# Eight row scatters behind the second routing half, and the v projection of the next chunk moved up behind q

## The chip, the cores and the metric

The program runs on one core of a Trainium2 chip. Its five instruction queues are TensorE (PE in the profile, PEld for its weight loads), VectorE (DVE), ScalarE (ACT), GpSimd (POOL) and SyncE (SP); they meet only at semaphores. The time is the device time of one execution in microseconds (us).

## The reference

The inputs are 8 sequences of 512 tokens with 256 features (4096 tokens). Each token is layer-normalised to `xn`. From it come two branches:

```
q, v   = xn @ Wq, xn @ Wv
state  = lam * state_before + v          # along the 512 tokens, lam = sigmoid(beta) per head
y      = layernorm(q * state) * ln_g + ln_b
s      = (y * silu(xn @ Wg)) @ Wo

logits = xn @ router.T                   # 8 experts, the best 2 of a token, softmax of the two
moe    = sum over the 2 experts e of gate_e * (silu(a) * b) @ w_out[e].T,  a, b = halves of xn @ w_in[e].T
out    = x + s * silu(moe + bias)
```

## The kernel before, in words

The work has three stages, each with its own instruction order per engine, written out by hand.

**Stage 1, normalise and route (0 to about 45 us).** The 8 sequences ("chunks") are normalised, transposed and projected on the 8 experts. The choice of two experts is made in two halves of 16 token tiles each: `choose(0)` on VectorE after chunks 0 to 3, `choose(1)` after chunks 4 to 7. Behind each choice, TensorE counts ranks (`count_ranks`), and VectorE turns them into a row number for every (token, expert) pair (`count`, `place`). `place(g)` signals `routed`; `choose(g)` signals `chosen_ready`.

**Stage 2, the recurrence (about 45 to 173 us).** It goes chunk by chunk, c = 0 to 7. VectorE runs the scan of v along the tokens (L910, signals `states_ready`), splits pieces of the expert weights (L919), multiplies by q (L923, signals `prod_ready`), multiplies by the gate (L954, L960), and takes the statistics of q * state (L936, L943, signals `y_var`). GpSimd makes the reciprocal standard deviation from them (`rstd`, L414 to L417, signals `y_rstd`). ScalarE normalises with it (L646, signals `z_ready`). TensorE transposes the result (`transpose_z`, L1134), ScalarE applies ln_g and ln_b (L605), and one chunk later the gate and the output projection follow (`project_out`). TensorE's accumulators are fixed: bank A holds v, bank B holds q, bank C the gate and the output projection by turns, bank D the transposes. So v of chunk c + 1 may be written only when the scan of chunk c has read bank A.

Beside this, GpSimd copies all token rows to their places in a list sorted by expert in DRAM: 64 scatters (L452), each of 128 rows, one for a token tile and one of its two experts. They are issued from GpSimd's own queue in batches between the calls of `rstd`: `SCATTERS_FIRST` of them ahead of chunk 0, then `SCATTERS_EACH` = 8 behind the `rstd` of each chunk, until 64 are out:

```
            done = SCATTERS_FIRST
            scatter(0, done)
            for c in range(CH):
                if c >= 1:
                    pool.wait_ge(z_ready, c)
                rstd(0, y_var, c + 1, y_rstd)
                end = min(done + SCATTERS_EACH, N_SCATTERS)
                scatter(done, end)
                done = end
```

With 14 first, chunks 0 to 5 carry 8 each, chunk 6 carries the last 2, and chunk 7 none. `scatter` waits for `routed` of the half that its rows belong to.

**Stage 3, the experts (from about 173 us).** SyncE waits until all 64 scatters have landed (`rows_scattered`) and loads the sorted rows block by block (L347). TensorE transposes a block (L1192), and runs the two layers of its expert as products of fp16 pieces (L1068, the helper `three`, which also makes all projections of stage 2). The results are scattered back with an add (L525), and after the last block the chunks are finished and stored.

Of the kernel before, what the change touches and what calls it, by code (L numbers as in the profile page):

```python
# [62 lines left out]
GROUPS = 2  # L63
# [4 lines left out]
MASKED = -3.0e38  # L68
ROWS_OUT = T + P
N_SCATTERS = TOPK * NT  # L70
SCATTERS_FIRST = 14
SCATTERS_EACH = 8


# [27 lines left out]
def build(nc, x, wq, wv, wg, wo, beta, ln_g, ln_b, router, w_exp, bias, out):  # L102
    ctx = ExitStack()
    with ctx:
# [84 lines left out]
        def routing(shape, dims, dt=F32, words=None):  # L189
# [46 lines left out]
        bankA, bankB, bankC, bankD = [  # L236
            ctx.enter_context(nc.psum_tensor(f"bank{n}", [P, 2, 512], F32)) for n in "ABCD"]
# [14 lines left out]
        def slots_ps_of(b, i):  # L252
# [13 lines left out]
        logits_done, route_step, chosen_ready, ranks_done = map(  # L266
            sem, ("logits_done", "route_step", "chosen_ready", "ranks_done"))
# [3 lines left out]
        v_ps, q_ps, g_ps, yt_ps, zt_ps, o_ps = map(  # L271
            sem, ("v_ps", "q_ps", "g_ps", "yt_ps", "zt_ps", "o_ps"))
        states_ready, prod_ready, ybn_done, y_var, y_rstd, z_ready = map(
            sem, ("states_ready", "prod_ready", "ybn_done", "y_var", "y_rstd", "z_ready"))
# [112 lines left out]
        def _(pool):  # L387
# [59 lines left out]
            def scatter(first, end):  # L447
                for a in range(first, end):
                    slot, row = scatters[a]
                    if a % (TOPK * GT) == 0:  # L450
                        pool.wait_ge(routed, a // (TOPK * GT) + 1)
                    pool.indirect_dma_start(  # L452
                        out=slots_dram, out_offset=bass.IndirectOffsetOnAxis(slot, 0),
                        in_=row, in_offset=None,
                        bounds_check=SLOTS - 1, oob_is_err=False).then_inc(rows_scattered, 16)


            done = SCATTERS_FIRST
            scatter(0, done)
            for c in range(CH):  # L460
# [87 lines left out]
        def _(act):  # L548
# [50 lines left out]
            def affine(c, buffers=early_buffers):  # L599
                _, w, _, _ = buffers  # L600
                act.wait_ge(zt_ps, c)
                if not isinstance(c, int) or c >= 2:
                    act.wait_ge(p_lo_ready, KD * (c - 1))
                for m in range(KD):
                    act.activation(w[:, m, :], bankD[:, m, :], ACT.Identity, bias=cols[:, 2, m:m + 1],  # L605
                                   scale=cols[:, 1, m:m + 1]).then_inc(w_ready, 1)

            def split_p(c, buffers=early_buffers):
                _, w, p_hi, _ = buffers
                if not isinstance(c, int) or c >= 2:  # L610
                    act.wait_ge(o_ps, c - 1)
                for m in range(KD):
                    act.wait_ge(p_ready, KD * (c - 1) + m + 1)
                    act.activation(p_hi[:, m, :], w[:, m, :], ACT.Copy).then_inc(p_hi_ready, 1)
# [105 lines left out]
        def _(dve):  # L720
# [181 lines left out]

            def recur(c, convert=True):
                states, _, _, _ = early_buffers
                later = not isinstance(c, int) or c >= 1
                dve.wait_ge(v_ps, c + 1)
# [156 lines left out]
        def _(pe):  # L1063
# [38 lines left out]
            def project_half(bank, a, c, m):  # L1102
                return three(bank[:, m, :], range(KD),
                             lambda k: wat_hi[:, a, k, m * P:m * P + P],
                             lambda k: wat_lo[:, a, k, m * P:m * P + P],
                             lambda k: xnT[:, bass.ds(c, 1), k, :].rearrange("p a n -> p (a n)"),
                             lambda k: xnT[:, bass.ds(c, 1), KD + k, :].rearrange("p a n -> p (a n)"))

            def project(bank, a, c):
                project_half(bank, a, c, 0)  # L1110
                return project_half(bank, a, c, 1)
# [18 lines left out]
            def transpose_z(c):  # L1130
                pe.wait_ge(z_ready, c)
                for j in range(TPC):
                    for m in range(KD):
                        last = pe.transpose(bankD[:, m, j * P:j * P + P], z[:, j, m * P:m * P + P],  # L1134
                                            ident32[:, :])
                last.then_inc(zt_ps, 1)

            def project_out(c):
                _, _, p_hi, p_lo = early_buffers
                pe.wait_ge(p_lo_ready, KD * c)  # L1140
                for j in range(TPC):
                    last = three(bankC[:, j // 2, j % 2 * D:j % 2 * D + D], range(KD),
                                 lambda k: p_hi[:, k, j * P:j * P + P],
                                 lambda k: p_lo[:, k, j * P:j * P + P],
                                 lambda k: wat_hi[:, 3, k, :],
                                 lambda k: wat_lo[:, 3, k, :])
                last.then_inc(o_ps, 1)

            def recur(c, last=False):

                states, _, _, _ = early_buffers
                later = not isinstance(c, int) or c >= 1
                if later:
                    pe.wait_ge(prod_ready, c)
                project(bankB, 0, c).then_inc(q_ps, 1)
                if later:
                    transpose_z(c)
                if not isinstance(c, int) or c >= 2:
                    pe.wait_ge(s_ready, c - 1)
                if later:  # L1160
                    project(bankC, 2, c).then_inc(g_ps, 1)
                pe.wait_ge(prod_ready, c + 1)
                if later:
                    pe.wait_ge(w_ready, KD * c)
                for j in range(TPC):
                    for m in range(KD):
                        y_t = pe.transpose(bankD[:, j // 2, j % 2 * D + m * P:j % 2 * D + m * P + P],  # L1167
                                            states[:, m, j * P:j * P + P], ident32[:, :])
                y_t.then_inc(yt_ps, 1)
                if not last:  # L1170
                    pe.wait_ge(states_ready, c + 1)
                    project(bankA, 1, c + 1).then_inc(v_ps, 1)
                if later:
                    pe.wait_ge(gate_ready, c + 1)
                    project_out(c)

            project(bankA, 1, 0).then_inc(v_ps, 1)
            count_ranks(1)
            repeat(pe, 1, CH - 1, 1, recur)
            recur(CH - 1, last=True)  # L1180


# [148 lines left out]
```

## Time and profile before

| what | us |
|---|---|
| median of 3 runs (lowest, highest) | 524.18 (521.8, 524.3) |
| the profiled execution, its own time | 526.04 |
| its span in the trace | 524.3 |
| TensorE busy in the span | 431.1 (82%) |
| VectorE busy | 305.7 (58%) |
| GpSimd busy | 273.8 (52%) |
| ScalarE busy | 214.8 (41%) |

All times of rows count from the start of the span. A row of the timeline gives the start, the busy time, the engine, the source line, the operation, what it writes and reads, and in brackets how long the engine sat idle ahead of it and what released it. "issue" means that nothing in the profile released it, "remote" that a semaphore rose with no instruction's end beside it. Line numbers are those of the kernel before; in the changed kernel the lines behind L457 stand one to four lines lower.

### The profile page before, as it was taken

To read this page: it belongs to the slowest core of one execution; us is meant where nothing else is said; L and a number is where in the kernel's file an instruction comes from. 1 tells how busy PE (TensorE), PEld (TensorE's weight loads), DVE (VectorE), ACT (ScalarE), POOL (GpSimd) and SP (SyncE) were. 2 spreads that over 40 slices of the span, in tenths; PEclk is the share of its full clock that TensorE was granted. 3 is DMA by queue.
4 is the path that set the end of the run, shared out by engine and by line. 5 is a ranking of instruction groups with operands and counts; after the bars stand their busy time and mean duration, and the time that the engine had idled before them with its cause. 6 is when DMAs were issued, how large, how long until landed. Compare 5 with 4: busy or idle time off the path is not lost.

```text
span 524.3 us, 12044 instructions
## 1 busy us (share of the span) xinstructions
PE 431.1 (82%) x3446; PEld 339.5 (65%) x3447; DVE 305.7 (58%) x589; ACT 214.8 (41%) x340; POOL 273.8 (52%) x524
## 2 busy tenths in 40 slices
PE   1766389699699989999899998999999999998000
PEld 1643245465355878888798887888888888765000
DVE  4897489889687445454445453545545454444067
ACT  4872136558565534243323333333434243232050
POOL 4716377477885206555555655564646556543300
PEclk9999689799899999999999999999999999999755
DMA  7802143996892224565434333434334343442398
GB/s 252 301 12 83 61 163 139 316 290 231 280 325 96 66 81 62 141 140 106 61 57 63 68 50 62 70 59 71 52 69 60 61 60 57 68 64 30 71 334 306
DMA packets 52692, 64.70 MB, mean 123 GB/s; under 512 B 5552, under 2 KB 47536, under 8 KB 52656
## 3 DMA queue, kind: packets, MB, share of 16 engines
q1 hardware_dynamic: 37712, 45.55, 28.1%
q0 software_dynamic: 13296, 17.83, 20.3%
q10 hardware_dynamic: 1664, 1.06, 0.7%
q8 instruction: 10, 0.16, 0.1%
q14 instruction: 10, 0.08, 0.0%
HBM read 40.02 MB, written 28.74 MB: 131 GB/s over the span
## 4 chain that ended last, share of the span: by engine, by line
PE 48%; DMA 13%; DVE 11%; issue 11%; POOL 8%; ACT 3%; another core or an unknown queue 2%; SPq 2%; DVEq 0%; POOLq 0%; ACTq 0%
PE bankC L1068 16%; PE bankB L1068 14%; PE bankA L1068 14%; DMA y_dram<-rows_raw 8%; POOL slots_dram L452 4%; PE bankD L1192 3%; DMA w_raw<-x_in 2%; DMA rows_raw<-slots_dram 2%; DMA w_raw<-y_dram 1%; DVE w_raw L919 1%; POOL stat L416 1%; DVE work L910 1%; DVE w_raw L1046 1%; DVE bn L735 1%
## 5 line engine op out<-in xcount | busy, mean ns | idle before, releaser
L525 POOL DMA_INDIRECT y_dram<-rows_raw x71 | 113.3, 1596 | 31.3 <-issue 31.3
L1068 PE MATMUL bankC<-w_raw,rows_raw 128*128 x852 | 99.6, 273 | 2.2 <-DVE rows_raw L1038 2.2
L1068 PEld LDWEIGHTS bankC<-w_raw,rows_raw 128*128 128x128 f16 x852 | 82.0, 98 | 14.0 <-issue 3.3
L1068 PE MATMUL bankA<-rows_raw,w_raw 128*128 128x256 f16 x768 | 89.1, 273 | 1.2 <-DVE rows_raw L975 1.2
L1068 PE MATMUL bankB<-rows_raw,w_raw 128*128 128x256 f16 x768 | 89.1, 273 | 0.0
L452 POOL DMA_INDIRECT slots_dram<-rows_raw,pos_i x64 | 72.1, 1127 | 31.2 <-issue 20.7
L1068 PEld LDWEIGHTS bankA<-rows_raw,w_raw 128*128 x768 | 75.0, 98 | 10.1 <-issue 1.4
L1068 PEld LDWEIGHTS bankB<-rows_raw,w_raw 128*128 x768 | 75.2, 98 | 8.3
L985 DVE TENSOR_TENSOR rows_raw<-rows_raw 128x512 f16<-128x512 f32 x64 | 44.3, 692 | 45.6 <-ACT rows_raw L673 45.6
L981 DVE SCALAR_TENSOR_TENSOR rows_raw<-rows_raw,bankA 128x512 f32<-128x512 f32 x32 | 22.0, 688 | 73.6 <-ACT rows_raw L668 73.6
L673 ACT ACTIVATE rows_raw<-rows_raw 128x512 f16<-128x512 f32 x64 | 40.3, 630 | 49.7 <-DVE rows_raw L981 49.7
L668 ACT ACTIVATE rows_raw<-bankA 128x512 f32<-128x512 f32 x32 | 19.1, 597 | 101.0 <-PE bankA L1068 67.6
L519 POOL TENSOR_TENSOR spare<-spare 128x1 f32<-128x1 f32 x32 | 6.2, 194 | 94.0 <-DVE rows_raw L1000 93.0
L1000 DVE TENSOR_SCALAR rows_raw<-bankC,rows_raw 128x256 f32<-128x256 f32 x71 | 31.4, 479 | 11.3 <-DMA y_dram<-rows_raw 9.3
L981 DVE SCALAR_TENSOR_TENSOR rows_raw<-rows_raw,bankB 128x512 f32<-128x512 f32 x32 | 22.0, 688 | 15.0 <-ACT rows_raw L668 15.0
L668 ACT ACTIVATE rows_raw<-bankB 128x512 f32<-128x512 f32 x32 | 19.1, 597 | 21.3 <-PE bankB L1068 21.3
L919 DVE SCALAR_TENSOR_TENSOR w_raw<-work,w_raw 128x1024 f32 (+1 forms) x24 | 27.7, 1216 | 0.0
L646 ACT ACTIVATE work<-bankD,stat 128x256 f32<-128x256 f32 x32 | 15.4, 565 | 23.7 <-POOL stat L417 23.6
L975 DVE TENSOR_TENSOR rows_raw<-bankD,rows_raw 128x512 f16<-128x512 f32 (+1 forms) x37 | 23.4, 633 | 2.5 <-ACT rows_raw L660 2.4
L618 ACT ACTIVATE w_raw<-work 128x1024 f32 (+1 forms) x24 | 23.5, 1046 | 1.9 <-DMA work<-w_exp_in 1.9
L1167 PE MATMUL bankD<-ident,work 128*128 128x128 f32 x64 | 10.5, 317 | 16.5 <-DVE work L923 16.5
L1192 PE MATMUL bankD<-ident,rows_raw 128*128 128x128 f32 x134 | 21.5, 278 | 3.1 <-DMA rows_raw<-slots_dram 3.0
(180 smaller groups left out, 664.5 us busy)
## 6 DMA issues: line engine op xcount, KB each, us to landing
work<-w_exp_in SPq DMA_DIRECT2D x24, 512.0 KB
rows_raw<-slots_dram SPq DMA_DIRECT2D x32, 260.0 KB
w_raw<-x_in SPq DMA_DIRECT2D x9, 512.0 KB, 4.2
y_dram<-bias_in SPq DMA_DIRECT2D x4, 1024.0 KB
w_raw<-y_dram SPq DMA_DIRECT2D x8, 512.0 KB, 7.3
out<-w_raw SPq DMA_DIRECT2D x8, 512.0 KB, 3.7
work<-x_in SPq DMA_DIRECT2D x7, 512.0 KB
slots_dram<-fill SPq DMA_DIRECT2D x9, 260.0 KB
```

Of the source, the lines that this page charges most:

```text
L452: pool.indirect_dma_start(out=slots_dram, out_offset=bass.IndirectOffsetOnAxis(slot, 0), in_=row, in_offset=None, bounds_check=SLOTS - 1, ...
L525: pool.indirect_dma_start(out=y_dram, out_offset=bass.IndirectOffsetOnAxis(to, 0), in_=ys[i][:, s, :], in_offset=None, bounds_check=ROWS_O ...
L618: act.activation(w_hi[:, bass.ds((c * PIECES + i) * PIECE, PIECE)], wst[:, i % STAGES, :], ACT.Copy, scale=WSCALE).then_inc(w_hi_ready, 1)
L668: act.activation(sil[j][:, :, 0:n], AB[j][:, :, 0:n], ACT.Silu, scale=1.0 / WSCALE).then_inc(sil_ready, 1)
L673: act.activation(g_hi[i][:, 2 * j:2 * j + 2, 0:n], g32[j][:, :, 0:n], ACT.Copy)\
L919: dve.scalar_tensor_tensor(w_lo[:, piece], wst[:, i % STAGES, :], WSCALE, w_hi[:, piece], ALU.mult, ALU.subtract).then_inc(w_lo_ready, 1)
L975: dve.tensor_tensor(xT[i][:, KD:2 * KD, 0:n], slots_ps_of(b, i)[:, :, 0:n], xT[i][:, 0:KD, 0:n], ALU.subtract).then_inc(slot_lo_ready, 1)
L981: dve.scalar_tensor_tensor(g32[j][:, :, 0:n], sil[j][:, :, 0:n], 1.0 / WSCALE, AB[j][:, :, BLOCK:BLOCK + n], ALU.mult, ALU.mult).then_inc( ...
L985: dve.tensor_tensor(g_lo[i][:, 2 * j:2 * j + 2, 0:n], g32[j][:, :, 0:n], g_hi[i][:, 2 * j:2 * j + 2, 0:n], ALU.subtract).then_inc(g_split, 1)
L1000: last = dve.tensor_scalar(ys[i][:, s, :], bankC[:, i, s * D:s * D + D], gates[:, s:s + 1], None, ALU.mult)
L1068: last = pe.matmul(out_ap, lhsT, rhs, start=(n == 0), stop=(n == len(todo) - 1))
L1192: last = pe.transpose(slots_ps_of(b, i)[:, k, s * P:s * P + P], slot_in[i][:, s, k * P:k * P + P], ident32[:, :])
```

## The change

Two places are edited. GpSimd waits for `chosen_ready` of both halves before its first scatter, and issues 8 instead of 14 there. On TensorE, the v projection of chunk c + 1 stands directly behind the q projection of chunk c, ahead of the transposes of z, the gate's projection and the transposes of q * state; before it stood behind all three.

```diff
-SCATTERS_FIRST = 14
+SCATTERS_FIRST = 8
 SCATTERS_EACH = 8
...
+            pool.wait_ge(chosen_ready, GROUPS)
             done = SCATTERS_FIRST
             scatter(0, done)
...
                 project(bankB, 0, c).then_inc(q_ps, 1)
+                if not last:
+                    pe.wait_ge(states_ready, c + 1)
+                    project(bankA, 1, c + 1).then_inc(v_ps, 1)
                 if later:
                     transpose_z(c)
...
                 y_t.then_inc(yt_ps, 1)
-                if not last:
-                    pe.wait_ge(states_ready, c + 1)
-                    project(bankA, 1, c + 1).then_inc(v_ps, 1)
                 if later:
                     pe.wait_ge(gate_ready, c + 1)
                     project_out(c)
```

GpSimd's queue around the first scatters and the first two chunks, before (`slots_dram` is the sorted list, `mv` and `stat` the statistics of a chunk, `x13` a run of like instructions):

```order
L452 DMA slots_dram<-rows_raw,pos_i 35072x260 [waits routed]
L452 DMA slots_dram<-rows_raw,pos_i 35072x260 x13
L414 TENSOR_SCALAR stat<-mv 128x4 [waits y_var]
L415 TENSOR_SCALAR stat<-mv 128x4
L416 TENSOR_TENSOR stat<-stat,neg_half 128x4 [waits pool_step]
L417 TENSOR_TENSOR stat<-stat 128x4 [waits pool_step]
L452 DMA slots_dram<-rows_raw,pos_i 35072x260 x8
L414 TENSOR_SCALAR stat<-mv 128x4 [waits y_var,z_ready]
```

And in the changed kernel:

```order
L452 DMA slots_dram<-rows_raw,pos_i 35072x260 [waits routed,chosen_ready]
L452 DMA slots_dram<-rows_raw,pos_i 35072x260 x7
L414 TENSOR_SCALAR stat<-mv 128x4 [waits y_var]
L415 TENSOR_SCALAR stat<-mv 128x4
L416 TENSOR_TENSOR stat<-stat,neg_half 128x4 [waits pool_step]
L417 TENSOR_TENSOR stat<-stat 128x4 [waits pool_step]
L452 DMA slots_dram<-rows_raw,pos_i 35072x260 x8
L414 TENSOR_SCALAR stat<-mv 128x4 [waits y_var,z_ready]
```

The first batch has one more wait and six scatters fewer; every later scatter moves back by six places, and the batch behind the `rstd` of chunk 6 grows from 2 to 8.

TensorE's queue in chunk 0, from the last q product on, before (bank B is q, bank A is v, bank D takes the transposes, `xs_raw` is the transposed input, `work` holds q * state):

```order
L1068 MATMUL bankB<-xs_raw,wat_hi 128x512 x2
L1068 MATMUL bankB<-xs_raw,wat_lo 128x512
L1167 MATMUL bankD<-ident,work 128x128 [waits prod_ready]
L1167 MATMUL bankD<-ident,work 128x128 x7
L1068 MATMUL bankA<-xs_raw,wat_hi 128x512 [waits states_ready]
L1068 MATMUL bankA<-xs_raw,wat_hi 128x512
L1068 MATMUL bankA<-xs_raw,wat_lo 128x512
```

And in the changed kernel, where the source lines have shifted:

```order
L1069 MATMUL bankB<-xs_raw,wat_hi 128x512 x2
L1069 MATMUL bankB<-xs_raw,wat_lo 128x512
L1069 MATMUL bankA<-xs_raw,wat_hi 128x512 [waits states_ready]
L1069 MATMUL bankA<-xs_raw,wat_hi 128x512
L1069 MATMUL bankA<-xs_raw,wat_lo 128x512
```

The 12 products of v(1) now follow those of q(0) and wait only for the scan; the 8 transposes, which wait for `prod_ready`, come behind them. In the loop over chunks 1 to 6 the same move is made past the transposes of z, the 12 products of the gate and the transposes of q * state.

## Rows read from the trace of the kernel before

**Rows 1.** Engine busy times by stretch: from:to, length, busy (instructions), PEclk, DMA, GB/s.

```profile
190.00:206.00 16.00, 16.00 (x147) 14.26 (x146) 7.34 (x13) 4.76 (x8) 6.83 (x15) 1.00 0.37 92
```

**Rows 2.** GpSimd's timeline: the scatters and the first rstd instruction of chunks.

```profile
40.86 1.26 POOL L452 DMA_INDIRECT slots_dram<-rows_raw,pos_i  x1 [10.55 <-DVE rows_raw L812]
...
57.80 0.98 POOL L452 DMA_INDIRECT slots_dram<-rows_raw,pos_i  x1 [0.30 <-issue]
66.50 0.24 POOL L414 TENSOR_SCALAR stat<-mv 128x4 f32<-128x4 f32 x1 [7.72 <-DVE mv L943]
...
80.89 0.24 POOL L414 TENSOR_SCALAR stat<-mv 128x4 f32<-128x4 f32 x1 [0.39 <-issue]
...
100.52 0.24 POOL L414 TENSOR_SCALAR stat<-mv 128x4 f32<-128x4 f32 x1 [5.92 <-DVE mv L943]
...
116.35 0.24 POOL L414 TENSOR_SCALAR stat<-mv 128x4 f32<-128x4 f32 x1 [1.89 <-DVE mv L943]
...
152.39 1.97 POOL L452 DMA_INDIRECT slots_dram<-rows_raw,pos_i  x1 [0.30 <-issue]
...
161.30 0.24 POOL L414 TENSOR_SCALAR stat<-mv 128x4 f32<-128x4 f32 x1
...
163.79 1.10 POOL L452 DMA_INDIRECT slots_dram<-rows_raw,pos_i  x1 [0.54 <-issue]
165.19 0.97 POOL L452 DMA_INDIRECT slots_dram<-rows_raw,pos_i  x1 [0.30 <-issue]
```

**Rows 3.** VectorE's timeline, stages 1 and 2.

```profile
39.70 0.17 DVE L812 TENSOR_SCALAR rows_raw<-w_raw 128x16 f32<-128x16 f32 x1
...
45.27 0.42 DVE L770 TENSOR_REDUCE w_raw<-bankD 128x128 f32<-128x256 f32 x1 [2.77 <-remote]
...
54.51 0.17 DVE L844 TENSOR_TENSOR_SCAN w_raw<-w_raw 128x8 f32<-128x8 f32 x1
61.19 1.22 DVE L923 SCALAR_TENSOR_TENSOR work<-bankB,work 128x1024 f32<-128x1024 f32 x1 [6.51 <-remote]
...
66.13 0.28 DVE L943 BATCH_NORM_AGGREGATE mv<-bn 128x2 f32<-128x6 f32 x3
68.40 2.33 DVE L910 TENSOR_TENSOR_SCAN work<-cols,bankA 128x512 f32<-128x512 f32 x2 [1.99 <-PE bankA L1068]
...
102.30 2.33 DVE L910 TENSOR_TENSOR_SCAN work<-cols,bankA 128x512 f32<-128x512 f32 x2 [1.95 <-PE bankA L1068]
...
150.04 4.61 DVE L919 SCALAR_TENSOR_TENSOR w_raw<-work,w_raw 128x1024 f32 x4
...
164.84 1.22 DVE L923 SCALAR_TENSOR_TENSOR work<-bankB,work 128x1024 f32<-128x1024 f32 x1 [2.44 <-PE bankB L1068]
```

**Rows 4.** TensorE's timeline, the products whose ends others wait for.

```profile
42.55 0.56 PE L1087 MATMUL bankD<-rt,xs_raw 128*128 128x16 f16 x16 [0.29 <-DVE xs_raw L746]
...
54.15 0.38 PE L1068 MATMUL bankB<-xs_raw,wat_lo 128*128 128x512 f16 x1
...
104.61 0.27 PE L1068 MATMUL bankC<-wat_hi,work 128*128 128x256 f16 x1
```

**Rows 5.** ScalarE's timeline, the copy of the output projection of chunk 2.

```profile
107.46 1.02 ACT L623 ACTIVATE xs_raw<-bankC 128x1024 f32 x1 [3.03 <-remote]
```

**Rows 6.** SyncE's timeline: issue of the first two block loads.

```profile
168.46 1.55 SPq L347 DMA_DIRECT2D rows_raw<-slots_dram  x2
```

**Rows 7.** The chain of waits: 12 projection products, one block load (start, us, what).

```profile
104.89 2.59 PE bankB L1068 x12
...
313.98 2.72 DMA rows_raw<-slots_dram
```

**Rows 8.** TensorE's timeline: the first block's transposes and its first expert product.

```profile
172.83 1.04 PE L1192 MATMUL bankB<-ident,rows_raw 128*128 128x128 f32 x8
175.06 0.61 PE L1068 MATMUL bankA<-rows_raw,w_raw 128*128 128x256 f16 x4 [1.19 <-DVE rows_raw L975]
```

**Rows 9.** Engine busy times by stretch, behind TensorE's wait for q * state.

```profile
61.20:66.00 4.80, 3.53 (x13) 2.37 (x14) 4.62 (x16) 0.00 (x0) 0.00 (x0) 0.50 0.00 0
```

## The prediction

> **What bounds the kernel now.** I read the busy times by stretch first, then the timelines of GpSimd, VectorE and TensorE for stages 1 and 2. In stage 3 TensorE is busy without a gap, 16.00 of 16.00 us [rows 1], and neither edit touches it. So the question is only when stage 3 starts: its first expert product is at 175.06 [rows 8].
>
> In stage 2, GpSimd is the engine to follow. Call R(c) the start of the `rstd` of chunk c. R(0) to R(3) are 66.50, 80.89, 100.52 and 116.35, and R(6) is 161.30 [rows 2]. In front of R(2) and R(3) GpSimd stood idle for 5.92 and 1.89 us, released by VectorE's statistics. In front of R(1) the idle time is 0.39 us, and R(6) shows none: there the eight scatters of the chunk before set the pace. From R(3) to R(6), 44.95 us, I take it that scatters set it.
>
> The start is set by something else. The statistics of chunk 0 end at T0 = 66.13 + 0.28 = 66.41 [rows 3], and two waits ahead of them are marked "remote". Routing L770 starts at 45.27 although its last product ended at 42.55 + 0.56 = 43.11 [rows 3, 4]: 2.2 us late. The product L923 starts at 61.19, although VectorE was free at 54.68 and the last q product ended at 54.53 [rows 3, 4]: 6.7 us after it. By the code L923 waits for nothing but q and the scan, so TensorE's signal itself arrived late. The only other work that runs through both waits is the 14 scatters, 40.86 to 58.78 [rows 2], and L923 starts 2.4 us after the last one was issued. A third case is ScalarE's copy at 107.46, 2.6 us behind a product that ended at 104.88 [rows 4, 5], also among scatters. But L923 of chunk 7 starts 0.0 us after the q product that released it, with a scatter running at 163.79 [rows 2, 3]. So scatters go with late signals, but not always. In the two shorter cases TensorE had more work queued behind the signal; in the 6.7 us case its next instruction waited for VectorE.
>
> **The change, part by part.**
>
> *No scatters during the second choice.* L770 can start at about 43.2, 2.1 us earlier, and everything behind it on VectorE moves along: the choice, which ended at about 50.0, ends at 47.9, and VectorE is free for L923 at 54.68 - 2.1 = 52.6 instead of 61.19. GpSimd's first scatter began 0.99 us after its release (39.70 + 0.17 to 40.86 [rows 2, 3]), so the new first one begins at 48.9. The pace is (57.80 - 40.86) / 13 = 1.30 us; eight take 7 x 1.30 + 0.98 = 10.1, with 0.3 for the longer first, to 59.3.
>
> *T0.* With no late signal, L923 moves from 61.19 to 52.65, and T0 from 66.41 to 57.9. But q of chunk 0 now ends inside the scatters again. The lower bound of the lateness is 0 (chunk 7), the upper one is "2.4 us after the last scatter", L923 at 61.7. I take one delay of 2.4 us, the mean of 2.2 and 2.6, because v(1) now stands behind q(0) on TensorE, as other work did in the two shorter cases. T0 = 60.3. GpSimd is then free at 59.3, so it does not bind.
>
> *v moved up.* VectorE's scan waited 1.99 us at 68.40 and 1.95 at 102.30 for v [rows 3], because v stood behind the transposes. Now v is ready when VectorE gets there, and both waits go. What is late next? R(1) follows from the scatters, R(0) + 14.4. R(2) follows from VectorE: before 100.52 = T0 + 34.1, now T0 + 32.1; scatters would allow T0 + 28.2 (94.60 - 66.41). R(3) was T0 + 49.9, now less both waits, T0 + 46.0; scatters give T0 + 32.1 + 13.9 = T0 + 46.0, the same. From there the scatters set the pace, and a further wait removed is worth nothing: R(6) = T0 + 46.0 + 44.95 = T0 + 91.0, against T0 + 94.9 before.
>
> What stands behind the moved v on TensorE is the transposes of z. If v waits for the scan, they wait too: 2.6 us for v [rows 7], 1.04 for the transposes [rows 8], 0.8 on ScalarE, 4.4 in all behind the scan. VectorE needs the result only after L919 and L923, 4.61 + 1.2 = 5.8 us behind the same scan [rows 3]. The cover is 1.4 us, so I price the move at zero; a TensorE at half clock would use the cover up and cost about 2 us in that chunk, which GpSimd's pace mostly hides from chunk 3 on.
>
> *Six scatters moved back.* Before, chunk 6 carried two, and the last was issued by S = 165.19 + 0.97 = 166.16. Now it carries eight: 2.49 us of `rstd` (161.30 to 163.79) and 10.1 of scatters, so S = R(6) + 12.6 = T0 + 103.6, against T0 + 99.75. The block loads wait for it: SyncE issued the first 2.30 us after S [rows 6], and a load takes 2.7 us [rows 7], so TensorE transposes block 0 from S + 5.0, and the first expert product follows as before 2.1 us behind the end of waiting: S + 7.1 = T0 + 110.7. Before it was T0 + 108.65, and the loads were then hidden by the recurrence. So at an unchanged T0 this part costs 2.0 us: 3.9 from v gained, 5.9 lost to the scatters.
>
> A rule bears on the moved scatters. The scatter at 152.39 took 1.97 us instead of 0.98, beside L919 on VectorE from 150.04 for 4.61 us [rows 2, 3]. The Trainium skill (SBUF — State Buffer, section "SBUF: two separate sides") says that GpSimd and a VectorE instruction with two SBUF inputs lock each other out of a shared port pair for a whole instruction. By it, the six scatters leave a stretch where VectorE has little of that kind and enter chunk 7, where L954 and L960 are such instructions. The sum would be some 1 us worse if one scatter there doubles; chunk 7 has no L919, and I leave it out.
>
> *Clock.* TensorE now runs out of work at R(6) + 11.5 (172.83 - 161.30), T0 + 102.5, and gets block 0 at T0 + 108.6, an idle stretch of 6.1 us that was not there. After the idle stretch behind q(0) it was granted 0.50 of its clock, the 1.2 GHz level [rows 9]. Bounds: 0, or the transposes and the first 24 products (1.04 + 24 x 0.11 = 3.6, by four of them in 0.61 us, the last taking 0.27 [rows 8]) at double time, 3.6 us. I take 1.5, nearer the lower end, since these products also wait for copies on ScalarE and VectorE.
>
> **Sum.** T0 60.3 - 66.4 = -6.1; scatters against v +2.0; clock +1.5. Total -2.6 us. The profiled execution's own time is 526.04, 1.9 above the median of 524.18: I expect 523.4 for an execution like it, and 524.18 - 2.6 = 521.6 for the median.
>
> **Rivals.**
> - *No signal is late any more* (scatters in a row of eight leave TensorE's signals alone, as in chunk 7). T0 = 57.9, so -8.5 + 3.5 = -5.0: 519.2. Against it: two of three late signals came with fewer than eight scatters out.
> - *The signal waits for the end of the scatters.* L923 at 61.7, 0.5 later than before, T0 66.9, so +0.5 + 3.5 = +4.0: 528.2. For it: the 6.7 us case ended only once the scatters were out. This path is slower from T0 = 62.9 on, that is, when the signals cost over 5.0 us.
> - *The late signals have nothing to do with scatters.* Then L770 and L923 stay where they are and only the 3.5 us of the other parts remain: 527.7.
> - *The last batch hides after all* (clock at no cost, loads faster): -2.6 - 2.0: 519.6.
>
> **How the numbers follow.** Chances: forecast 0.42, no lateness 0.20, end of the scatters 0.23, no link 0.08, hidden batch 0.07. The forecast's own range is 519.5 to 524, by its clock bounds and a delay of 0 to 4 us. About 0.5% (2.6 us) is what a measurement of this kernel can tell from no change, and the forecast lies on that edge: half of it counts as faster. Faster 0.21 + 0.20 + 0.06 = 0.47; slower: most of the two cases above 527, 0.24; the same 0.29. The range is 518.0 to 528.3, which leaves out little more than the tails of the rivals.
>
> **What would show it.** Right: L770 within 0.2 us of its last product; L923 between 52.6 and 56; no wait of L910 for bank A; R(3) to R(6) still about 45 us; eight scatters behind R(6); a new TensorE idle stretch of some 6 us ahead of the first block's transposes, with SyncE's loads directly behind the last scatter. Wrong: L923 still near 61 us, or the block loads issued before TensorE ends the recurrence, which would mean that GpSimd does not set the end of stage 2.

## The result, and the profile after

Over 20 executions of each kernel the median went from 524.07 to 525.34 us; the ratio is 1.0055, 95% interval 1.0029 to 1.008. The two medians alone give 1.0024 and the two means 1.0044, so the size of the loss is known only roughly; its interval leaves out 1. Ratios leave out executions of a slower state, the medians given here keep them. The forecast was 521.6: the change is slower, not faster. The profiled execution of the changed kernel took 524.37 us (span 522.6), against 526.04 and 524.3 for the one that the prediction was worked out from. That pair says -1.7 where the medians say +1.3, so one pair of profiles does not settle it. The times of before lie in two groups (518.8 to 520.5 and, mostly, 523 to 526.5), those of the changed kernel between 522 and 527.7.

GpSimd's timeline in the changed kernel: first and last scatter of the first batch, R(0), R(2), R(3), R(6), last scatter of all.

```profile
48.77 1.26 POOL L452 DMA_INDIRECT slots_dram<-rows_raw,pos_i  x1 [18.39 <-DVE w_raw L782]
...
58.14 0.97 POOL L452 DMA_INDIRECT slots_dram<-rows_raw,pos_i  x1 [0.30 <-issue]
59.18 0.24 POOL L414 TENSOR_SCALAR stat<-mv 128x4 f32<-128x4 f32 x1
...
92.17 0.24 POOL L414 TENSOR_SCALAR stat<-mv 128x4 f32<-128x4 f32 x1 [3.91 <-DVE mv L944]
...
106.50 0.24 POOL L414 TENSOR_SCALAR stat<-mv 128x4 f32<-128x4 f32 x1
...
150.55 0.24 POOL L414 TENSOR_SCALAR stat<-mv 128x4 f32<-128x4 f32 x1
...
162.49 0.97 POOL L452 DMA_INDIRECT slots_dram<-rows_raw,pos_i  x1 [0.30 <-issue]
```

VectorE's timeline there: first routing step of the second half, product of chunk 0, end of its statistics, and the gate product of chunk 2.

```profile
43.06 0.42 DVE L771 TENSOR_REDUCE w_raw<-bankD 128x128 f32<-128x256 f32 x1 [0.65 <-PE bankD L1088]
...
52.59 1.22 DVE L924 SCALAR_TENSOR_TENSOR work<-bankB,work 128x1024 f32<-128x1024 f32 x1
...
57.59 0.28 DVE L944 BATCH_NORM_AGGREGATE mv<-bn 128x2 f32<-128x6 f32 x3
...
87.50 1.36 DVE L955 TENSOR_TENSOR work<-work 128x512 f32<-128x512 f32 x2 [1.65 <-ACT work L606]
```

Both waits that were "remote" in [rows 3] are gone: L771 follows its product at once (it was L770 at 45.27), and the product, at 61.19 before, starts at 52.59 without a wait. T0 is 57.87 instead of 66.41. R(0), at 59.18, now follows the last of the eight scatters directly: GpSimd, not T0, sets it.

SyncE's issue of the block loads, then TensorE's first transposes and expert products, and the stretch in which they lie (columns as in [rows 1]):

```profile
165.79 6.85 SPq L347 DMA_DIRECT2D rows_raw<-slots_dram  x4
```

```profile
168.65 1.11 PE L1193 MATMUL bankB<-ident,rows_raw 128*128 128x128 f32 x4 [5.20 <-DMA rows_raw<-slots_dram]
...
170.14 1.12 PE L1193 MATMUL bankB<-ident,rows_raw 128*128 128x128 f32 x4 [0.38 <-DMA rows_raw<-slots_dram]
...
171.38 4.23 PE L1069 MATMUL bankA<-rows_raw,w_raw 128*128 128x256 f16 x24
```

```profile
168.60:175.40 6.80, 6.25 (x32) 4.42 (x33) 1.38 (x2) 3.93 (x7) 2.16 (x12) 0.58 0.39 110
```

The last scatter's row ends at S = 163.46, the loads 2.33 us later. TensorE waits 5.20 us for them and then runs at a granted clock of 0.58 over this stretch, 0.50 being the 1.2 GHz level; the 24 first expert products take 4.23 us instead of the 2.79 of a kernel that arrives without the gap (e3 below). The first of them starts 20.83 us behind R(6), against 13.76 before [rows 2, 8].

| profiled execution | R(0) | R(0) to R(6) | R(6) to first expert product | from there to the span's end | span |
|---|---|---|---|---|---|
| before, forecast from it | 66.50 | 94.80 | 13.76 | 349.24 | 524.3 |
| before, second look (e3) | 62.87 | 91.06 | 13.74 | 349.43 | 517.1 |
| changed | 59.18 | 91.37 | 20.83 | 351.22 | 522.6 |
| changed, second look (f1) | 59.09 | 92.55 | 20.48 | 351.78 | 523.9 |

Against the first look the change wins 7.3 us up to R(0) and 3.4 from there to R(6), and gives back 7.1 and 2.0. Against the second it wins 3.7 and nothing, gives back 8.9, and loses 5.5.

### The profile page after: what moved, and what is told of

Read it like the earlier page. It is cut to its first block, busy times and chain, and to the rows that moved or that the text cites. A ratio compares the mean times of both kernels' runs of the same rounds, so it can differ in the third digit from the quotient of the medians.

```text
span 522.6 us, 12045 instructions
## 1 busy us (share of the span) xinstructions
PE 431.3 (83%) x3446; PEld 339.4 (65%) x3447; DVE 306.9 (59%) x589; ACT 214.9 (41%) x340; POOL 274.8 (53%) x524
## 4 chain that ended last, share of the span: by engine, by line
PE 44%; issue 16%; POOL 14%; DMA 14%; DVE 8%; SPq 2%; ACT 2%; POOLq 1%; DVEq 0%; ACTq 0%
PE bankC L1069 14%; PE bankB L1069 14%; PE bankA L1069 12%; POOL slots_dram L452 9%; DMA y_dram<-rows_raw 8%; PE bankD L1193 3%; POOL stat L416 2%; DMA rows_raw<-slots_dram 2%; DMA w_raw<-x_in 2%; DVE w_raw L1047 1%; DMA w_raw<-y_dram 1%; DVE bn L736 1%; POOL stat L415 1%; POOL y_dram L526 1%; SPq L365 1%
## 5 line engine op out<-in xcount | busy, mean ns | idle before, releaser
L1069 PE MATMUL bankA<-rows_raw,w_raw 128*128 128x256 f16 x768 | 90.5, 275 | 0.1
L1001 DVE TENSOR_SCALAR rows_raw<-bankC,rows_raw 128x256 f32<-128x256 f32 x71 | 31.4, 480 | 10.9 <-DMA y_dram<-rows_raw 8.8
L1069 PE MATMUL bankA<-xs_raw,wat_hi 128*128 (+1 forms) x64 | 20.9, 410 | 8.1 <-DVE work L911 8.1
L1069 PE MATMUL bankC<-wat_hi,work 128*128 128x256 f16 x128 | 22.4, 273 | 4.5 <-DVE work L961 2.2
L477 POOL TENSOR_TENSOR rows_raw<-rows_raw,blk_e 128x2 f32<-128x2 f32 x32 | 23.8, 742 | 3.4 <-DMA rows_raw<-slots_dram 3.3
```

Of the source, the lines that this page charges most:

```text
L477: pool.tensor_tensor(is_first[i][:, :], slot_in[i][:, :, D], e_b, ALU.subtract)\
L1001: last = dve.tensor_scalar(ys[i][:, s, :], bankC[:, i, s * D:s * D + D], gates[:, s:s + 1], None, ALU.mult)
L1069: last = pe.matmul(out_ap, lhsT, rhs, start=(n == 0), stop=(n == len(todo) - 1))
```

## The experiments

The experiments stand on four chips, one for each set below; a kernel is compared with the kernel before on its own chip. That median was 523.9 in the first set and 519.5, 519.1 and 519.0 in the others; the changed kernel was at 525.3 in the result and at 524.6 in the third set.

**First set: the parts of the change one by one.**

e3, no edit.

> The kernel before, unchanged, profiled a second time. Its 20 times so far lie in two groups, six between 518.8 and 520.5 and most of the rest between 523.9 and 526.5, 5 us apart. Theory A (the late signal ahead of L923 is in most executions, and its absence makes the lower group): a profile of about 526 shows L923 some 6 us behind the last q product again, one of about 520 shows it directly behind. Theory B (the late signal was a thing of that one profiled execution): L923 stands directly behind q, near 54.7, at any time. An execution of 525 or more with L923 near 54.7 speaks against A.

Over its 8 executions the unchanged kernel came out at 1.0023 of itself (0.9977 to 1.007): a ratio of that size is noise in this set. The profiled execution took 518.9 us, and it is neither theory. VectorE's timeline in it, TensorE's transposes, and GpSimd's R(0) and R(6):

```profile
42.87 0.42 DVE L770 TENSOR_REDUCE w_raw<-bankD 128x128 f32<-128x256 f32 x1 [0.65 <-PE bankD L1087]
...
52.44 1.22 DVE L923 SCALAR_TENSOR_TENSOR work<-bankB,work 128x1024 f32<-128x1024 f32 x1
...
60.94 1.43 DVE L936 BATCH_NORM_STATS2 bn<-bankD 128x6 f32<-128x256 f32 x4 [4.85 <-remote]
```

```profile
53.72 1.97 PE L1167 MATMUL bankD<-ident,work 128*128 128x128 f32 x8 [3.20 <-issue]
...
165.44 1.04 PE L1192 MATMUL bankB<-ident,rows_raw 128*128 128x128 f32 x8
...
167.67 2.79 PE L1068 MATMUL bankA<-rows_raw,w_raw 128*128 128x256 f16 x24 [1.19 <-DVE rows_raw L975]
```

```profile
62.87 0.24 POOL L414 TENSOR_SCALAR stat<-mv 128x4 f32<-128x4 f32 x1 [4.25 <-DVE mv L943]
...
153.93 0.24 POOL L414 TENSOR_SCALAR stat<-mv 128x4 f32<-128x4 f32 x1
```

L923 is on time here, but now it is the transposes of q * state (53.72 to 55.69) whose signal reaches L936 at 60.94, 5.25 us late. The late signal is there again, on another instruction, and T0 is 62.78 instead of 66.41. The other 3.7 us between the two looks lie between R(0) and R(6), with v where it always was.

e1, only v moved:

```diff
                 project(bankB, 0, c).then_inc(q_ps, 1)
+                if not last:
+                    pe.wait_ge(states_ready, c + 1)
+                    project(bankA, 1, c + 1).then_inc(v_ps, 1)
...
-                if not last:
-                    pe.wait_ge(states_ready, c + 1)
-                    project(bankA, 1, c + 1).then_inc(v_ps, 1)
```

> Only the v projection is moved; 14 scatters first and no new wait, as before. By the sum on record the move saves 3.9 us up to chunk 3, and nothing is lost to the scatters or the clock: 0.9925 of before. If the late signal of q(0) also shrinks from 6.7 to 2.4 us because v now stands behind q: 0.985. Rival: the move is worth nothing, because the transposes of z now wait behind v and the scatters set the pace all the same: 1.000, and the change's loss is all from the scatters.

1.0052 (1.0015 to 1.0088), median 524.35: not 0.9925. Whether it is worse than the rival's 1.000 is less sure, since the median lies only 0.5 us above that of the kernel before and the unchanged kernel had 1.0023. The late signal is there (VectorE waits 5.80 us, and L923 starts 5.1 us behind the last q product, although v(1) is queued behind it), and in chunk 7 VectorE waits 4.31 us for ScalarE's L605, against 1.14 and 2.82 in the two looks at before:

```profile
59.54 1.23 DVE L923 SCALAR_TENSOR_TENSOR work<-bankB,work 128x1024 f32<-128x1024 f32 x1 [5.80 <-remote]
...
164.35 1.36 DVE L954 TENSOR_TENSOR work<-work 128x512 f32<-128x512 f32 x2 [4.31 <-ACT work L605]
```

e2, only the scatters: the wait added, `SCATTERS_FIRST = 8`, v in its old place.

> Only the scatters are changed (the wait, and 8 first); v stays behind the transposes. By the sum on record: the scatters' end +5.9 us, the clock +1.5, and the earlier end of chunk 0's statistics -6.1: +1.3 us, 1.0025. If most executions of before have no late signal (theory B), the -6.1 is missing: +7.4 us, 1.014. If the late signal is typical and goes entirely (theory A): -8.5 in place of -6.1, 0.998.

1.0063 (1.0025 to 1.01), median 525.41, 1.5 us above the kernel before where the sum gave 1.3. The ratio lies between the forecast's 1.0025, at the edge of its interval, and the 1.014 for a kernel before without late signals, and it excludes 0.998. The end of chunk 0's statistics on VectorE, then R(0) and R(6) on GpSimd, then the first expert products on TensorE:

```profile
57.11 0.28 DVE L944 BATCH_NORM_AGGREGATE mv<-bn 128x2 f32<-128x6 f32 x3
```

```profile
58.74 0.24 POOL L414 TENSOR_SCALAR stat<-mv 128x4 f32<-128x4 f32 x1
...
151.00 0.24 POOL L414 TENSOR_SCALAR stat<-mv 128x4 f32<-128x4 f32 x1
```

```profile
171.62 5.30 PE L1069 MATMUL bankA<-rows_raw,w_raw 128*128 128x256 f16 x24 [0.17 <-DVE rows_raw L976]
```

T0 is 57.39, and the first expert product comes 20.62 us behind R(6). This is the changed kernel without v's move, and it is like the changed kernel in these: R(0) to R(6) 92.26 us against 91.37 and 92.55, ratio 1.0063 against 1.0055. The two were not run side by side, each against the kernel before.

e4, the changed kernel with `SCATTERS_FIRST = 14` again, behind the wait.

> The changed kernel with 14 scatters again in the first batch, still behind the choice of the second half. The first rstd then waits for them, to about 67 (48.8 + 13 x 1.30 + 1.3), as late as before, but the last batch is two scatters again: block loads hidden behind the recurrence, no idle TensorE ahead of the first block. If the scatters' end and the clock are what the change pays (3.5 us at an unchanged T0, theory B's whole loss), this kernel is 2 to 4 us faster than the changed one: 0.994 to 0.999 of before. Rival: the loss is in the late start of scatters itself (GpSimd's total work is one queue, and 8 us of it now start 8 us later): then it is as slow as the changed kernel or slower, 1.005.

1.0089 (1.0053 to 1.0125), median 526.87: the expectation fails. T0 is 57.8, but GpSimd reaches R(0) only behind its 14 scatters, at 68.12:

```profile
67.07 0.98 POOL L452 DMA_INDIRECT slots_dram<-rows_raw,pos_i  x1 [0.30 <-issue]
...
68.12 0.24 POOL L414 TENSOR_SCALAR stat<-mv 128x4 f32<-128x4 f32 x1
```

The tail is short again (13.76 us), so 7.1 us gained there are less than the 9 lost ahead of R(0). Whoever holds scatters back for the choice pays where they end.

**Second set: what the end of the scatters costs, and v in three places.** e5 is the changed kernel with `SCATTERS_EACH = (8, 11, 8, 8, 8, 8, 8, 8)`. e7 adds to it three scatters ahead of the wait; e8 is e7 with v behind `transpose_z(c)`, e9 is e7 with v in its old place.

```diff
+            scatter(0, SCATTERS_AHEAD)
             pool.wait_ge(chosen_ready, GROUPS)
-            done = SCATTERS_FIRST
-            scatter(0, done)
+            done = SCATTERS_AHEAD + SCATTERS_FIRST
+            scatter(SCATTERS_AHEAD, done)
```

> The changed kernel with 11 scatters instead of 8 behind the rstd of chunk 1, where GpSimd stood idle for 3.9 us ahead of R(2), so that the last batch is 5 instead of 8. If the loss is the late end of the scatters and the half clock behind it: the last scatter, the loads and the first expert product 3.9 us earlier, the TensorE gap 1.3 instead of 5.2 us, and up to 1.9 us less at half clock: 4 to 6 us below the changed kernel's 525.3, so 519.5 to 521.4 or 0.992 to 0.995 of before. Rival (the loss is spread over the chunks, by v's new place or by late signals): 1.003 to 1.005, as the changed kernel.

522.47, 1.0057 (1.0029 to 1.0084): the expectation fails. In its profile S moves only from 163.46 to 161.86, since the chunks take longer (R(0) to R(6) 94.0 us). More than half of the tail goes all the same: 16.4 us instead of 20.8, the first 24 expert products in 2.79 us, and 348.8 to the end.

> As e5, and three more scatters ahead of the wait for the choice, from about 41, where GpSimd is idle for 8 us; the last batch is then 2, as in the kernel before. The end of the scatters hides behind the recurrence and stage 3 starts 13.8 us behind R(6) as in the kernel before: R(6) stays near 150.6, the first expert product at 164.3 instead of 171.4, and no half clock: 516 to 518, 0.985 to 0.988 of before. If three scatters are enough to make TensorE's signal to L771 late (2.2 us): 518 to 520.

> As e7, with v of the next chunk behind the transposes of z and ahead of the gate's projection. Theory: with v directly behind q, the transposes of z are late and VectorE's L955 waits for ScalarE's L606 (10.0 us in four waits of the changed kernel), which eats the 4 us that the waits for v had cost. Then this place keeps both short: 1 to 3 us faster than e7. Rival: GpSimd's scatters set the pace of all chunks whatever the order on TensorE: within 0.2% of e7.

> As e7, with v in its old place behind the transposes of q * state. By the sum on record v's new place saves 3.9 us: this kernel 0.7% slower than e7. By the run with v alone (1.005 of before): 0.5% faster than e7. By scatters that set the pace: the same.

e7 521.27, 1.0023 (0.9991 to 1.0054); e8 521.30, 1.0028 (1.001 to 1.0046); e9 518.38, 0.998 (0.9953 to 1.0006). The tail is hidden in all three (13.7 to 14.8 us), but e7 misses the 516 to 520 expected. e8 does not beat e7: from 60 to 165 us, L957's waits for L608 fall from 10.9 to 2.4 us, and waits of L939 for the transposes of q * state, 8.5 us, take their place. The old place is the best of the three, by 2.9 us in the medians and 2.2 in the ratios (e7 to e9).

**Third set: the changed kernel beside one with a hidden tail.** f2 is the changed kernel with six scatters ahead of the wait (`SCATTERS_AHEAD = 6`, 8 in each later batch); f5 is f2 with v in its old place.

> The changed kernel, unedited, beside the kernels of this call on one chip. Where the kernel before runs mostly in its lower group (519.5, as in the call with e5 to e9), its late signal costs it less, and the changed kernel loses more: 1.007 to 1.01. Where it runs at 524: 1.003 to 1.008 as so far. Its profile should show L924 without a wait, R(6) near 151 and the first expert product 20.8 us behind R(6).

> The changed kernel with six more scatters ahead of the wait for the choice, from 41 to 48.6, where GpSimd is idle; from the wait on the first batch and the later ones are the same, and the last batch is 2 instead of 8, as in the kernel before. This prices the end of the scatters and the half clock alone. By the profile of the changed kernel: first expert product 13.8 to 15 us behind R(6) instead of 20.8, the rest 349.3 instead of 351.2: 8 us less, 0.985 of f1. If six scatters make L771 late by 2.2 us and chunk 0 by another 2 to 5: 2 to 6 us less than f1. If the end of the scatters costs nothing: as f1.

> As f2, with v in its old place: the kernel before with its first 14 scatters split 6 and 8 around the choice. By e7 against e9 it is 0.3 to 0.5% faster than f2, and the version to beat the kernel before: the chunks' pace is that of the kernel before, without most of the 5 to 6.5 us of late signal in chunk 0: 0.990 to 0.998 of before. By the sum on record (v's new place saves 3.9 us): 0.7% slower than f2.

f1 524.62, 1.0094 (1.0057 to 1.013); f2 521.05, 1.004 (1.0012 to 1.0067); f5 517.97, 0.9976 (0.9952 to 1.0). On this chip the whole difference of the change, 5.5 us, is then: the tail 3.6 (f1 to f2, less a late signal that comes back), v's new place 3.1 (f2 to f5; 3.3 by the ratios), and the scatters' split around the choice -1.1 (before to f5). This way of splitting depends on its order: the 3.1 is v's price with scatters ahead of the choice, which the changed kernel does not have. In the profiles f2's tail is 8.3 us shorter than f1's (15.29 and 348.64 against 20.48 and 351.78), but its R(0) is 2.6 later, because a late signal is back in chunk 0. VectorE and GpSimd there in f2, and below it in f5:

```profile
59.75 1.42 DVE L939 BATCH_NORM_STATS2 bn<-bankD 128x6 f32<-128x256 f32 x4 [2.40 <-remote]
```

```profile
61.69 0.24 POOL L415 TENSOR_SCALAR stat<-mv 128x4 f32<-128x4 f32 x1 [1.82 <-DVE mv L946]
```

```profile
60.92 2.33 DVE L913 TENSOR_TENSOR_SCAN work<-cols,bankA 128x512 f32<-128x512 f32 x2 [2.54 <-remote]
```

```profile
59.22 0.24 POOL L415 TENSOR_SCALAR stat<-mv 128x4 f32<-128x4 f32 x1
```

With v directly behind q the transposes of q * state come later (in f2 they end at 57.14, in f5 at 55.41), their signal is the late one, and the statistics wait for it. With v last, the late signal is v's own; VectorE waits for it too, but R(0) does not. All four kernels with scatters ahead of the choice and v behind q in chunk 0 (e7, e8, f2, f7) show the first picture, all four with v last there (e9, f5, f6, f8) the second.

f3 and f4 take the scatters out of the chunks, `SCATTERS_EACH = (0, 0, 0, 0, 0, 0, 0, 56)`, with v last (f3) and v behind q (f4).

> Only the 8 scatters of the first batch run in the recurrence; the other 56 are issued behind the rstd of chunk 7, so stage 3 starts some 70 us later and only the pace of the chunks is read. v stands last, as before. It shows the pace of VectorE, ScalarE and TensorE where GpSimd does not set it, to be laid beside the same kernel with v behind q. With the sum on record the chunks here take 2 us more wherever VectorE waits for v: R(c) steps near 14; by the waits of the changed kernel, where L955 waits instead: both alike. No late signals are expected without scatters.

> The changed kernel with only the first 8 scatters in the recurrence, 56 behind the rstd of chunk 7 (stage 3 starts some 70 us later; only the chunks' pace is read). With v last the steps of R were 12.57, 19.65, 14.05, then 12.41 us each, and VectorE waited for v twice (1.4 and 1.7). By the sum on record the new place removes these waits: R(3) about 3 us earlier, steps of 12.4. If the transposes of z are late behind v: steps over 12.4 with waits of L955, and nothing gained.

GpSimd's timeline, R(3) to R(6) in f3 and then in f4, with VectorE's waits in f4 from 60 to 165 (total us, times, longest):

```profile
105.44 0.24 POOL L414 TENSOR_SCALAR stat<-mv 128x4 f32<-128x4 f32 x1 [12.13 <-DVE mv L944]
...
117.85 0.24 POOL L414 TENSOR_SCALAR stat<-mv 128x4 f32<-128x4 f32 x1 [10.49 <-DVE mv L944]
...
142.72 0.24 POOL L414 TENSOR_SCALAR stat<-mv 128x4 f32<-128x4 f32 x1 [10.54 <-DVE mv L944]
```

```profile
103.07 0.24 POOL L414 TENSOR_SCALAR stat<-mv 128x4 f32<-128x4 f32 x1 [10.85 <-DVE mv L944]
...
115.85 0.24 POOL L414 TENSOR_SCALAR stat<-mv 128x4 f32<-128x4 f32 x1 [10.85 <-DVE mv L944]
...
141.31 0.24 POOL L414 TENSOR_SCALAR stat<-mv 128x4 f32<-128x4 f32 x1 [10.76 <-DVE mv L944]
```

```profile
DVE work L955 <- ACT work L606: 2.0, 5, 0.9
```

Up to R(3) the move gains 2.4 us, as the sum had it in kind. Behind it a chunk takes 12.75 us with v behind q and 12.43 with v last (a third of the way from R(3) to R(6)): L955 now waits 0.2 us in two of the three, where it did not wait. And with scatters a chunk takes 14.7 us (the same third in the changed kernel), for GpSimd's sake, 2 us more than either.

**Fourth set: which chunks pay for v's new place.** f6 is f2 with v behind q in chunks 1 to 6 only (`if not last and later`), f7 in chunk 0 only, f8 is f5 again.

> As f2 (six ahead), but in chunk 0 v stays last, behind the transposes of q * state; in chunks 1 to 6 it is directly behind q. f2 was 3.1 us slower than f5. Theory C0 (the cost of v's new place is in chunk 0: with v ahead, the late signal falls on the transposes, on which the first statistics wait, R(0) at 61.7 instead of 59.2; with v last it falls on v, which nobody needs then): as f5, 0.3 to 0.5% faster than f2. Theory C7 (the cost is in the later chunks, the transposes of z behind v): as f2, 1.003 to 1.005 of before.

> The other half: v directly behind q in chunk 0 only, last in chunks 1 to 6. C0: as f2, R(0) near 61.7 and 1.003 to 1.005 of before. C7: as f5, 0.996 to 0.999.

> f5 unedited, as the anchor for f6 and f7 on one chip, and to see whether it stays ahead of the kernel before: 0.994 to 1.000, lower on a chip where the kernel before runs at 524. R(0) near 59.2 by the scatters, R(6) near 152, first expert product 13.7 us later.

f6 519.90, 1.0017 (0.9993 to 1.0042); f7 520.17, 1.000 (0.9977 to 1.0022); f8 518.75, 0.999 (0.9967 to 1.0012). The medians of both halves lie 1.2 and 1.4 us above f8, but the three intervals overlap and f2 ran on another chip: the times alone neither show a cost of either half nor tell which is dearer. The profiles show both mechanisms: R(0) is 62.60 in f7 (L939 waits 4.25 us) and 59.93 in f6, and from 60 to 165 us L957 waits 9.3 us for L608 in f6 and 4.2 in f7.

f5, f8 and e9 are 0.1 to 0.24% below the kernel before, each interval touching 1: no better version is shown, only one as fast with the tail hidden. On a chip where the kernel before runs at 524 none of them was run.

## Why the prediction was wrong

**The step that failed is "v moved up", -3.9 us.** In the changed kernel the move is worth nothing: R(0) to R(6) is 92.26 us without it (e2) and 91.37 and 92.55 with it, and the ratios to the kernel before are 1.0063 and 1.0055. The 3.4 us that the first pair of profiles shows there are not v's: the second look at the kernel before has 91.06 with v in its old place. Without this term the sum gives +1.3 us; the medians say +1.3, the ratio 2.9. In the kernels with the first batch split around the choice the new place costs 2.2 to 3.3 us (e7 to e9, f2 to f5), and only with no later scatters does it gain, 1.25 us from R(0) to R(6) (f3 to f4).

The sum removed the waits for v in [rows 3] and then wrote R(2) = T0 + 32.1 and R(3) = T0 + 46.0; measured are T0 + 34.3 and T0 + 48.6. The cover of 1.4 us, at which "I price the move at zero", is what broke. TensorE in chunk 2 of the changed kernel, the stretch of that v, and ScalarE's step behind it:

```profile
80.33 1.03 PE L1069 MATMUL bankA<-xs_raw,wat_hi 128*128 x2 [6.37 <-DVE work L911]
...
85.43 1.14 PE L1135 MATMUL bankD<-ident,work 128*128 128x128 f32 x8
```

```profile
80.40:85.40 5.00, 5.00 (x12) 1.89 (x13) 5.00 (x5) 0.00 (x0) 4.34 (x3) 0.50 0.65 209
```

```profile
86.69 1.45 ACT L606 ACTIVATE work<-bankD,cols 128x512 f32<-128x512 f32 x2 [7.88 <-issue]
```

v waits for the scan, which comes late in chunk 2 since VectorE makes the list of blocks first. TensorE has nothing else in front of it, idles 6.37 us, and runs v at the 1.2 GHz level: 5.1 us instead of the 2.6 of [rows 7]. The transposes of z, queued behind, start at 85.43, L606 at 86.69, and L955 waits 1.65 us (its row is above). Of the 1.99 us that the scan of chunk 1 no longer waits, nothing is left by R(2): T0 + 34.3, where the forecast was worked out from T0 + 34.1. The prediction had named this case, "a TensorE at half clock would use the cover up and cost about 2 us in that chunk", and dismissed it because GpSimd hides it; but GpSimd stood idle ahead of R(2) (3.91 us), so there it was in full view. The second cost, the late signal that falls on the transposes in chunk 0, was not thought of; it is in the kernels with scatters ahead of the choice and not in the changed one, where the signals of chunk 0 are on time.

**T0 was right in its direction and uncertain in its weight.** The late signals of chunk 0 go when the scatters start behind the choice, and T0 even falls to 57.87, the first rival's start, not 60.3. The reason given for a delay of 2.4 us, that v(1) stands queued behind q(0), does not hold: in e1 it stands there and the delay is 5.1. And "GpSimd does not bind" failed: R(0) is 59.18. And the 6.1 us were taken off one execution whose late signal was 6.7 us long and lay on q. In the second look R(0) lies 3.6 us earlier, and where the kernel before runs at 519, f5, which holds eight of the first 14 scatters back for the choice, is only 1.1 us ahead of it. On the chip of the first set, where the kernel before has a median of 523.9, e2 with its early T0 is still 0.6% slower by the ratio and 1.5 us by the medians: the gain did not pay for the tail there either. That the sum without v comes so near to these medians is in part luck, since the T0 it starts from is that of one execution.

**The tail was right in kind and 1.7 us short.** Forecast 5.9 for the scatters and 1.5 for the clock, 7.4 in all; measured 7.1 and 2.0 in the profiles, 9.1. None of the eight scatters of the last batch doubled (the longest took 1.26 us). From S to the first expert product it is 7.9 us instead of 7.1, since the second half of the block is transposed 1.5 us behind the first (the sum's 2.1 us behind the end of the wait were 2.2 in [rows 8], and are 2.7 here). Of the 2.0, the 24 products take 1.4 (4.23 against 2.79); the rest is within what that last stretch differs by among the kernels with a hidden tail (348.6 to 350.6). The gap of TensorE was forecast at 6.1 us and is 5.2, the loads come directly behind the last scatter, and the first products run at half clock. Of the two terms that were to outweigh it, the -3.9 is missing whole, and how much of the -6.1 is there seems to depend on how fast the kernel before runs: by the medians the change loses 1.3 us where that one runs at 524, and 5.5 where it runs at 519 (f1).

Of the rivals, the hidden last batch and the signal that waits for the end of the scatters are excluded for the changed kernel by these rows: L924 starts at 52.59, while the scatters run to 59.11. "No signal is late any more" is what the profile shows, but its 519.2 used the same gain for v. The time came nearest to the rival without a link (527.7), for another reason. What stays open is why the kernel before runs at 519 on three chips and at 524 on that of the first set and in the result, and how often its late signal falls on q.

## What to carry to other kernels

A stall of one profiled execution is not a term of the sum until a second profile of the same kernel shows it in the same place; here the second look was 7 us shorter. When work is moved up in a queue of which it waits for another engine, ask what now stands behind that wait and whether the queue's engine idles in front of it, since here the idling cost its clock too (6.37 us idle, then a granted clock of 0.50). And when two engines set the pace by turns, a wait removed on the faster one hands the time to the other: measure each pace alone first (12.4 us a chunk without scatters, 14.7 with them here).

## What the runs showed of the hardware

The late TensorE signals go with scatters. In all eleven profiles with scatters both ahead of and behind the choice (before twice, e1, e7 to e9, f2, f5 to f8), VectorE waits 2.2 to 6.5 us "remote" for one signal of chunk 0. In the seven where they begin behind it, at 48.3 to 48.8 (after, f1, e2, e4, e5, f3, f4), it does not. Whichever product the signal belongs to, in those eleven it arrives at about the end of the first batch, from 0.1 us before the last scatter of the batch ends (f2, e7, e8) to 2.4 behind it (before). In f2, whose transposes end at 57.14 and whose L939 starts at 59.75, that scatter is

```profile
58.90 0.97 POOL L453 DMA_INDIRECT slots_dram<-rows_raw,pos_i  x1 [0.30 <-issue]
```

So the prediction's rival of a signal that waits for the end of the scatters fits the eleven, though not the seven. What the wait costs then depends on which signal is hit: q puts T0 at 66.41 (before), the transposes at 62.78 (e3), v at 58.38 (f5). Later in the recurrence four of the eleven show one more, 2.7 to 3.4 us for v at 123 to 126 us (e3, f5, f7, f8). L770 of the choice waited so with two scatters out in two of the looks with 14 ahead (before, e1) and not in the third, so the number alone is not the rule, and it came in the midst of the batch. Why TensorE's signal waits is not shown.

A scatter can take 5.3 us instead of 0.97. GpSimd's and VectorE's timelines in f2:

```profile
84.11 5.34 POOL L453 DMA_INDIRECT slots_dram<-rows_raw,pos_i  x1 [0.30 <-issue]
```

```profile
84.01 4.59 DVE L922 SCALAR_TENSOR_TENSOR w_raw<-work,w_raw 128x1024 f32 x4
```

It stood beside all four L922 (L919 before), not one of them, and f7 has the like (5.33 us); no other scatter of the 18 profiles takes over 2.5. The Trainium skill (SBUF — State Buffer, section "SBUF: two separate sides") lets a VectorE instruction with two SBUF inputs and a GpSimd one that reads SBUF share a port pair, which whichever starts first keeps for its whole instruction. The trace agrees in kind, but by that rule the scatter would wait for one L922, an estimated 1.15 us (a quarter of 4.59), and this one ended 0.85 us behind the last of the four. Whether a lock held over four instructions in a row or something else delayed it is not shown. The commoner long scatter beside these instructions, as at 152.39 in [rows 2], is 1.97.
